# Head attention of a four-layer graph kernel: keys prepared before queries, and the head-stacking copies spread over three DMA queues

## What is computed

```
layer 0: three graph convolutions with layer norm       agg = adj^T (h W);  h = relu(LN(agg + b + h))
layer 1: additive attention (GAT)                        softmax(a . relu(q_i + k_j) + mask) @ h
layer 2: head attention, 4 heads of 32
         Q = h Wq + bq,  K = h Wk + bk,  V = h Wv + bv
         S = Q K^T / sqrt(32) + (1 - adj) * -1e9         per head, 2048 x 2048
         out = softmax(S) V  (heads side by side) @ Wo + bo
layer 3: normalised adjacency                            D^-1/2 (A + I) D^-1/2 h B
```

## Time and profile before

| | us |
|---|---|
| median of 3 runs | 13312.75 (13290.18 to 13324.34) |
| the profiled execution, its own time | 13312.38 |
| its span, first to last instruction | 13310.6 |
| PE busy in the span | 12569.7 (94%) |
| DVE busy | 10012.5 (75%) |
| ACT busy | 9177.3 (69%) |
| POOL busy | 372.5 (3%) |

### The profile page before, as it was taken

How to read it: one execution, slowest core, us unless ns; L and a number is a source line. 1 busy time by engine, 2 the same in 40 slices (tenths; PEclk the granted TensorE clock), 3 DMA queues, 4 the chain that set the end, 5 groups by cost and what they waited for, 6 DMA issues and landing times.

```text
span 13310.6 us, 251575 instructions
## 1 busy us (share of the span) xinstructions
PE 12569.7 (94%) x110721; PEld 6208.8 (47%) x110721; DVE 10012.5 (75%) x13975; ACT 9177.3 (69%) x8953; POOL 372.5 (3%) x500
## 2 busy tenths in 40 slices
PE   8998999989999899998999989999899998999989
PEld 3333843338433384333843338433384334843348
DVE  4887748877488775887758877598765887658876
ACT  3886738867388673886638866388663886638866
POOL 0000000000000000000000000000000000000000
PEclk9999999999999999999999999999999999999999
DMA  1001210012100131001310013100130001300012
GB/s 71 17 20 45 96 64 17 20 45 103 57 17 20 45 105 55 17 20 48 111 45 17 20 48 118 38 20 17 52 122 31 20 17 52 131 23 20 17 54 88
DMA packets 126942, 647.66 MB, mean 49 GB/s; under 512 B 15264, under 2 KB 49824, under 8 KB 52128
## 3 DMA queue, kind: packets, MB, share of 16 engines
q1 hardware_dynamic: 92688, 420.78, 9.3%
q0 software_dynamic: 20880, 143.66, 3.0%
q10 hardware_dynamic: 12288, 67.13, 2.2%
HBM read 556.01 MB, written 8.39 MB: 42 GB/s over the span
## 4 chain that ended last, share of the span: by engine, by line
PE 88%; DVE 6%; ACTq 2%; DMA 2%; ACT 1%; issue 1%; POOL 0%; SPq 0%; DVEq 0%
PE ps L1013 50%; PE ps L997 10%; PE ps L1055 8%; PE ps L1068 4%; PE ps L1026 4%; PE ps L1046 4%; PE ps L1185 3%; PE ps L949 2%; ACTq L535 2%; DMA adj_ring<-in_adj 1%; PE ps L1173 1%; DVE E L673 1%; DVE E L674 1%; DVE E L675 1%; DVE PT L701 1%
## 5 line engine op out<-in xcount | busy, mean ns | idle before, releaser
L1013 PE MATMUL ps<-E,a_win 128*32 128x512 f32 x65536 | 7113.6, 594 | 72.2 <-DVE E L675 72.2
L1013 PEld LDWEIGHTS ps<-E,a_win 128*32 128x32 f32 x65536 | 2102.5, 110 | 4904.7 <-issue 4745.5
L432 ACT ACTIVATE E<-Q,ka 128x2048 f32<-128x2048 f32 x2048 | 4073.5, 1989 | 0.0
L673 DVE TENSOR_SCALAR E<-Q,kd 128x2048 f32<-128x2048 f32 x2048 | 2628.8, 1284 | 794.3 <-PE ps L1013 757.8
L431 ACT ACTIVATE E<-Q,ka 128x1024 f32<-128x1024 f32 x2048 | 2347.9, 1146 | 964.9 <-PE ps L1013 964.3
L674 DVE TENSOR_SCALAR E<-Q,kd 128x2048 f32<-128x2048 f32 x2048 | 2623.2, 1281 | 0.0
L675 DVE TENSOR_SCALAR E<-Q,kd 128x1024 f32<-128x1024 f32 x2048 | 1531.0, 748 | 0.0
L742 DVE CUSTOM_DVE_ANT_0 T<-ps,adj_ring 128x2048 f32<-128x2048 f32 x512 | 1173.3, 2292 | 237.5 <-PE ps L1046 211.1
L459 ACT ACTIVATE T<-T,nmin 128x2048 f32<-128x2048 f32 x512 | 1022.1, 1996 | 316.1 <-issue 313.6
L371 ACT ACTIVATE PT<-ps 128x512 f32<-128x512 f32 x1792 | 1001.0, 595 | 341.6 <-PE ps L1055 276.9
L1055 PE MATMUL ps<-ident,T 128*128 128x128 f32 x8192 | 1128.5, 281 | 12.3 <-ACT PT L371 5.4
(11 more groups left out here) (119 smaller groups left out, 7590.5 us busy)
## 6 DMA issues: line engine op xcount, KB each, us to landing
adj_ring<-in_adj SPq DMA_DIRECT2D x384, 1024.0 KB, 4.9
adj_res<-in_adj POOLq DMA_DIRECT2D x128, 1024.0 KB, 7.4
qst<-qh ACTq DMA_DIRECT2D x64, 256.0 KB, 7.0
qst<-ql ACTq DMA_DIRECT2D x64, 256.0 KB, 8.7
kst<-kh ACTq DMA_DIRECT2D x64, 256.0 KB, 5.2
kst<-kl ACTq DMA_DIRECT2D x64, 256.0 KB, 5.2
HW<-in_x POOLq DMA_DIRECT2D x9, 1024.0 KB, 12.3
X<-in_x SPq DMA_DIRECT2D x128, 64.0 KB, 1.9
```

The source lines that it names most:

```text
L432: nc.scalar.activation(E[:, s + 3, :], Q2[:, :], ACT.Relu, bias=ka[:, u, 48 + m:49 + m]).then_inc(e_act, 1)
L673: nc.vector.tensor_scalar(E[:, s, :], Q2[:, :], kd[:, u, m:m + 1], 0.0, ALU.add, ALU.max)
L1013: last = mm(ps[QROWS * grp:QROWS * (grp + 1), 4 * u + c, :], win, E[:, s + grp, c * CH:(c + 1) * CH], start=(m == 0), stop=(m == QUADS - 1 ...
```

## The change

- The keys are projected, evacuated and split before the queries. DVE splits the keys in four chunks of 512 columns as ACT evacuates them, and the queries in two parts: `FIRST`, columns 0 to 511 (the first four tiles), and `REST`, the other 1536.
- The 16 key copies move to SP's queue, behind a wait for the fourth key chunk (`k2_dve`) and behind the first two ring loads of the head attention. ACT's queue copies only `FIRST` of the queries (16 DMAs of 64 KB). POOL's queue copies `REST` (16 DMAs of 192 KB), and only then issues `fetch`.
- The first score waits for `FIRST` of the queries (`stq_first`), not for all; `stq_rest` is waited for before tile 4's queries are taken. The wait for `V` moves from before the first score to before the third.
- `qh` and `ql` no longer lie under `T2`; `T2`'s heads 0 and 1 lie over an unused space.
- The `bo` addition moves from DVE to POOL, behind `fetch`; DVE waits for it (`bo_rdy`) where it adds the attention's output.
- The next graph's statistics move from before the first score into tiles 6 to 9, one `bn_stats` a step, and the aggregation into tile 10.

```diff
+        def stack(eng, dst, parts, h, cols, done):
+            for blk in range(4):
+                eng.dma_start(dst[HD * blk:HD * (blk + 1), h, cols].bitcast(F32),
+                              parts[blk][HD * h:HD * (h + 1), cols].bitcast(F32)).then_inc(done, 16)
+        FIRST, REST = slice(0, CH), slice(CH, N)
...
+                        if phase == 1 and tt == 0:
+                            sp.wait_ge(k2_dve, (b + 1) * NC)
+                            for h in range(HEADS):
+                                stack(sp, kst, (kh, kl, kh, kl), h, slice(0, N), stk_in[h])
...
-                pool.wait_ge(qk2_dve, b * 2 + 1)
+                pool.wait_ge(q2_dve, (b + 1) * 2)
+                for h in range(HEADS):
+                    stack(pool, qst, (qh, qh, ql, ql), h, REST, stq_rest)
                 fetch(b + 1 if more else b)
+                pool.wait_ge(zn_rdy, (b + 1) * (HEV * NC))
+                nc.gpsimd.tensor_tensor(X[:, :, :], X[:, :, :], over_tiles(bo_b[:, :]), ALU.add).then_inc(bo_rdy, 1)
...
-                for dst, parts, k in ((qst, (qh, qh, ql, ql), 1), (kst, (kh, kl, kh, kl), 2)):
-                    act.wait_ge(qk2_dve, b * 2 + k)
-                    for h in range(HEADS):
-                        for blk in range(4):
-                            act.dma_start(...)
+                act.wait_ge(q2_dve, b * 2 + 1)
+                for h in range(HEADS):
+                    stack(act, qst, (qh, qh, ql, ql), h, FIRST, stq_first)
...
                     if h == 1 and not last:
+                        if t == TPC - 1:
+                            dve.wait_ge(stq_rest, (b + 1) * (16 * 16))
                         queries2(b, t + 1, 1 - u)
...
-                nc.vector.tensor_tensor(X[:, :, :], X[:, :, :], over_tiles(bo_b[:, :]), ALU.add)
-                for src, hi, lo, k in ((HW, qh, ql, 0), (AGG, kh, kl, 1)):
...
+                for c in range(NC):
+                    cols = slice(c * CH, (c + 1) * CH)
+                    dve.wait_ge(k2_act, b * NC + c + 1)
+                    nc.vector.tensor_copy(kh[:, cols], AGG[:, cols]).then_inc(k2_hi, 1)
+                    dve.wait_ge(k2_hi, b * NC + c + 1)
+                    nc.vector.tensor_tensor(kl[:, cols], AGG[:, cols], kh[:, cols].bitcast(F32), ALU.subtract
+                                            ).then_inc(k2_dve, 1)
+                for k, cols in enumerate((FIRST, REST)):
+                    dve.wait_ge(q2_act, b * NC + (1, NC)[k])
+                    nc.vector.tensor_copy(qh[:, cols], HW[:, cols]).then_inc(q2_hi, 1)
+                    dve.wait_ge(q2_hi, b * 2 + k + 1)
+                    nc.vector.tensor_tensor(ql[:, cols], HW[:, cols], qh[:, cols].bitcast(F32), ALU.subtract
+                                            ).then_inc(q2_dve, 1)
...
-                stats_next(b + 1)
-                dve.wait_ge(stq_in, (b + 1) * (16 * 16))
+                dve.wait_ge(stq_first, (b + 1) * (16 * 16))
...
+                            k = ((tt - 3) * 2 + u) * HEADS + h
+                            if 0 <= k < NT:
+                                stats_of_next(b + 1, k)
+                            if k == NT:
+                                aggregate_next(b + 1)
...
-                pe.wait_ge(v_sb, (b + 1) * NC)
-                pe.wait_ge(qk2_act, (b + 1) * 8)
+                pe.wait_ge(q2_act, (b + 1) * NC)
...
+                        if t * HEADS + h == 2:
+                            pe.wait_ge(v_sb, (b + 1) * NC)
                         step2(b, S0 + t * HEADS + h, t, h, t, t * HEADS + h)
```

More of the change, by code:

```diff
@@ L46 @@
 LN_MID = LN_COUNT - 2
-DVE_STEPS = 66
+DVE_STEPS = 64
 STEPS = NT * HEADS
@@ L157, in build @@
             PT2 = sb("PT2", [P, NC, CH], where=ph)
+            qh = sb("qh", [P, N], F32R, where=ph)
+            ql = sb("ql", [P, N], F32R, where=ph)
             with ExitStack() as sub:
@@ L160, in build @@
             with ExitStack() as sub:
-                qh = sb("qh", [P, N], F32R, where=sub)
-                ql = sb("ql", [P, N], F32R, where=sub)
+                T2_front = sb("T2_front", [P, 2, N], where=sub)
                 kh = sb("kh", [P, N], F32R, where=sub)
@@ L215, in build @@
         x2_rdy = sem("x2_rdy")
-        qk2_ps = sem("qk2_ps")
-        qk2_act = sem("qk2_act")
-        qk2_dve = sem("qk2_dve")
+        k2_ps = sem("k2_ps")
+        k2_act = sem("k2_act")
+        k2_hi = sem("k2_hi")
+        k2_dve = sem("k2_dve")
+        q2_ps = sem("q2_ps")
+        q2_act = sem("q2_act")
+        q2_hi = sem("q2_hi")
+        q2_dve = sem("q2_dve")
+        bo_rdy = sem("bo_rdy")
         v_ps = sem("v_ps")
         v_sb = sem("v_sb")
-        stq_in = sem("stq_in")
+        stq_first = sem("stq_first")
+        stq_rest = sem("stq_rest")
         stk_in = [sem(f"stk_in{h}") for h in range(HEADS)]
@@ L252, in build, with over_tiles @@
         block = ctx.enter_context(nc.Block())
+        def stack(eng, dst, parts, h, cols, done):
[3 more added lines that the diff above has]
+        FIRST, REST = slice(0, CH), slice(CH, N)
         def alone(eng):
             eng.sem_inc(waited, 1)
+        def over_tiles(row):
+            return row.rearrange("p (o d) -> p o d", o=1).broadcast_to([P, NT, D])
         def tcols(t):
@@ L408, in evac_q2, with evac_k2 @@
             def evac_q2(b, c):
-                act.wait_ge(qk2_ps, b * 8 + c + 1)
-                nc.scalar.activation(HW[:, c * CH:(c + 1) * CH], ps[:, 4 + c, :], ACT.Identity,
-                                     bias=bqs_c[:, 0:1], scale=-SCALE).then_inc(qk2_act, 1)
+                act.wait_ge(q2_ps, b * NC + c + 1)
+                nc.scalar.activation(HW[:, c * CH:(c + 1) * CH], ps[:, c, :], ACT.Identity,
+                                     bias=bqs_c[:, 0:1], scale=-SCALE).then_inc(q2_act, 1)
+            def evac_k2(b, c):
+                act.wait_ge(k2_ps, b * NC + c + 1)
+                nc.scalar.activation(AGG[:, c * CH:(c + 1) * CH], ps[:, 4 + c, :], ACT.Identity,
+                                     bias=bk_c[:, 0:1]).then_inc(k2_act, 1)
             def degrees(b, t, T, half, u):
@@ L523, in _ @@
                 evac1(b * NT + NT - 1, 1)
-                h_section(b, 1, LAYERS, Hf, lambda c: evac_q2(b, c))
+                h_section(b, 1, LAYERS, Hf, lambda c: evac_k2(b, c))
                 for c in range(NC):
-                    act.wait_ge(qk2_ps, b * 8 + 4 + c + 1)
-                    nc.scalar.activation(AGG[:, c * CH:(c + 1) * CH], ps[:, c, :], ACT.Identity,
-                                         bias=bk_c[:, 0:1]).then_inc(qk2_act, 1)
-                for dst, parts, k in ((qst, (qh, qh, ql, ql), 1), (kst, (kh, kl, kh, kl), 2)):
-                    act.wait_ge(qk2_dve, b * 2 + k)
-                    for h in range(HEADS):
-                        for blk in range(4):
-                            act.dma_start(dst[HD * blk:HD * (blk + 1), h, :].bitcast(F32),
-                                          parts[blk][HD * h:HD * (h + 1), :].bitcast(F32)
-                                          ).then_inc(stq_in if k == 1 else stk_in[h], 16)
+                    evac_q2(b, c)
+                act.wait_ge(q2_dve, b * 2 + 1)
+                for h in range(HEADS):
+                    stack(act, qst, (qh, qh, ql, ql), h, FIRST, stq_first)
                 S0 = b * (NT * HEADS)
@@ L656, in tiles @@
                 return buf[:, :].rearrange("p (t d) -> p t d", t=NT)
-            def over_tiles(row):
-                return row.rearrange("p (o d) -> p o d", o=1).broadcast_to([P, NT, D])
             def keys(t, T, u, first):
@@ L808, in stats_next, with stats_of_next, aggregate_next @@
             def stats_next(n):
-                dve.wait_ge(xn_in, (n + 1) * 16)
-                XN = tiles(HW)
                 for t in range(NT):
-                    last = nc.vector.bn_stats(stats[:, t, :], XN[:, t, :])
-                last.then_inc(xn_bn, 1)
-                dve.wait_ge(xn_bn, n + 1)
+                    stats_of_next(n, t)
+                aggregate_next(n)
+            def stats_of_next(n, t):
+                if t == 0:
+                    dve.wait_ge(xn_in, (n + 1) * 16)
+                nc.vector.bn_stats(stats[:, t, :], tiles(HW)[:, t, :]).then_inc(xn_bn, 1)
+            def aggregate_next(n):
+                dve.wait_ge(xn_bn, (n + 1) * NT)
                 alone(dve)
@@ L915, in _ @@
                         xg = X[:, g * TPC:(g + 1) * TPC, :]
+                        dve.wait_ge(bo_rdy, b + 1)
                         last = nc.vector.tensor_tensor(xg, ps[:, 4 + g, :].rearrange("p (t d) -> p t d", d=D), xg,
@@ L1133, in _ @@
                 h_section(b, 1, LAYERS, lambda c: mm(
-                    ps[:, 4 + c, :], wq[:, :], HT[:, c * CH:(c + 1) * CH], start=True, stop=True).then_inc(qk2_ps, 1))
+                    ps[:, 4 + c, :], wk[:, :], HT[:, c * CH:(c + 1) * CH], start=True, stop=True).then_inc(k2_ps, 1))
                 for c in range(NC):
```

(5 more changed lines are left out.)

4 lines of the change are left out of this document (removed).

## The result

The changed kernel takes 13428.77 us (median of 4 runs, 13407.34 to 13444.71), the kernel before 13308.23 (4 runs on the same chip): ratio 1.0086, 95% interval 1.0074 to 1.0097. The medians are 120 us apart, 15 us a graph. The forecast was 13306, within 13225 to 13355: wrong, and outside its range. The profiled execution was the slowest of the four, with a span of 13442.9 us.

The account below looks back on a forecast made before the run. PE, busy 94% of the span, was taken as the bound, its waits for key copies as the place to save. First score +57 plus 18.3 us gave fifth score +75.3 against 76.0; times eight, -6 us: 13306, range 13225 to 13355.

Parts of the forecast that it names:

- The sharing: In the stacking, three queues take equal packet turns whatever the size; keys in at +54.5, first score at +58.2.
- rival 2: First score waits for nearly all stacking bytes, at +64.1; fifth at +82.4, +6.4 us a graph, 13363; chance 0.13.
- The rate: How fast engines carry the stacking: 212 GB/s within one half, 274 mixed; first score at +57 (55 to 59).
- mixed halves: Stacking copies reading both partition halves run at 274 GB/s, not 212, saving 2.3 us; half of that was taken.
- the loss side: Chance 0.15 of a result over 0.3% (40 us, 5 us a graph) slower than before.
- Rival 1: Queries get through the stacking early, first score about +41; keys then decide, -8 us a graph, 13249; chance 0.32.

Follow-up runs that it names:

- e1: The changed kernel, but POOL waits for all sixteen key copies to land before issuing REST and the fetch; 13273.34 us, ratio 0.9963 to the kernel before.
- e7: The changed kernel with ACT's and POOL's jobs swapped: POOL issues FIRST, then the fetch, and ACT issues REST; 13288.58 us, ratio 0.9976 to the kernel before.
- e5: As e3, but the key copies of heads 1 and 2 alternate in SP's queue; 13216.79 us, ratio 0.9921 to the kernel before.
- e4: The kernel before with only bo on POOL and the statistics in tiles 6 to 10, stacking untouched; 13324.94 us, ratio 1.0003.
- e3: The changed kernel, but SP alone issues head 0's keys, FIRST, other keys; POOL waits for the keys; 13220.16 us, ratio 0.9922 to the kernel before.
- e6: As e3, but ACT issues FIRST of heads 2 and 3 beside SP's of heads 0 and 1; 13173.66 us, ratio 0.9889 to the kernel before.

## Why the prediction was wrong

**The sharing: this step failed.** "That is one turn each, whatever the size" was read off one overlap and carried over to three queues. Between SP and ACT it is right: 386 to 342 packets in e1. POOL's queue is another matter: 325 packets to 143 and 128 in the changed kernel, 411 to 145 and 117 in e7.

The overlap that the forecast leaned on shows it, when its packets are counted in short stretches and not worked out from the whole. The queues of the kernel before, graph 2, from 4594 to 4604:

```profile
q10 hardware_dynamic: 232, 1.29, 60.0%
q0 software_dynamic: 271, 1.05, 39.8%
```

from 4596 to 4601:

```profile
q0 software_dynamic: 239, 0.96, 71.1%
q10 hardware_dynamic: 59, 0.30, 24.0%
```

and from 4597 to 4599:

```profile
q0 software_dynamic: 113, 0.46, 96.6%
q10 hardware_dynamic: 2, 0.01, 2.0%
```

The whole looks like near one for one, because ACT's queue has the engines to itself before the fetch flows and after most of it is through. In between the fetch took four packets for one. The forecast's working let the fetch flow 1.5 us after its issue and so gave it 11 us; its first packet came 3.5 us after the issue, at 4596.0, and 90% of its packets had started 5.2 us later. The stacking moved 1.29 MB in the ten microseconds, not 1.6. Graph 0 was read the wrong way round too: its fetch took longer, but drew 251 packets to the stacking's 186 from 1273 to 1283. In all eight graphs the first 244 packets of the fetch went beside only 41 to 161 of the stacking. So neither three queues nor a backlog of seventeen transfers is needed for the advantage; one transfer of POOL's beside one other queue has it.

The forecast quoted the Trainium skill for its rule ("DMA: Bandwidth & Descriptors", Queues, rings and completion order). But that section's packet is a bundle of some 9 to 17 descriptors, while the forecast took it for one packet of the profile; how the two relate, no run here shows. What the trace does show is that the fetch and the stacking did not change places packet by packet: 113 to 2 in 2 us are on average seven of the fetch's packets for each engine, with next to none of the other queue's between. A turn that carries more for POOL than for the others would fit all the counts; the size of a turn was not shown.

What it did to the order: the forecast had `FIRST` land "last but for `REST`", at +57.6. In fact it landed behind `REST` too, with the fetch. That is rival 2 ("If the turns favour POOL, `FIRST` lands with the end"), with its mechanism as written; it had been given 0.13, because SP would be "done by +55". By the forecast's own prices the order alone moves the first score from +57 to +64, seven of the twelve microseconds.

**The rate: a term mis-sized.** The other five are the rate. Rival 2's sum has 36.1 + 4.0 = 40.1 us for all 9.44 MB, which is 235 GB/s. From 1270 to 1314 the three queues moved 9.18 MB at 209 GB/s; at that rate 9.44 MB take 45.2 us. About 1.5 us of the difference stood in the rows before the change: there the bytes took 41.6 us (43.4 less 1.8), as the engines were not busy all the time. The rest is the price of a row. From 1276 to 1288 the 0.78 MB of SP are 95 rows of 8 KB and took 0.325 x 12 x 16 = 62.4 us of engine time, 0.66 each with the counting packets; POOL's 225 rows of 6 KB took 115.4, 0.51 each; ACT's 78 rows of 2 KB took 13.2, 0.17 each. The forecast had 0.56, 0.42 and 0.14. They are 18 to 22% dearer in this stretch, in which 2.32 MB took 12 us (193 GB/s). Why a row costs more was not shown.

The forecast had gone the other way, and taken 1.2 us off for mixed halves. Its reading of the earlier trace rows does not hold: in the stretch at 212 GB/s heads 1 and 2 met as well (ACT issued head 1's last key copy at 4620.54 and head 2's first at 4621.92, and such a copy is in flight for 6 us or more). e5 puts the gain at 4%, which is near the Trainium skill's 6% and far from the forecast's 274 to 212.

**The range.** The forecast gave the loss side 0.15 and ended the range at 13355, below its own rival 2 (13363). The fifth score's delay cost (87.7 - 76.0) x 8 = 94 us, where rival 2 had priced it at 51.

**What was right.** SP's first issue at +22.1; ACT at +24.5 (forecast 25.2), POOL at +28.3 (28.0). The fifth score 18.45 us after the first in graph 0 (18.9 in the mean), 18.3 forecast. No key wait of a minimum. SP's issues over at +51.9, before its ring load. ACT free for its first exp: it then waits 48.5 us for the minimum. `bo` takes 4.51 us on POOL, covered, and the statistics fit into tiles 6 to 10: e4 shows 1.0003 for both. "POOL's 16 issues delay only the fetch" was the sentence that hid the loss: they cost POOL 8 us, and took the engines from `FIRST`.

**Rival 1** (queries early, 13249) needs no luck with the sharing: e3 and e6 pass its time by keeping POOL's bytes back and ordering the rest by hand. The third minimum then waits for the keys, as it said: up to 6.1 us in e3, 5.2 in e6.

## What to carry to other kernels

Here, splitting a transfer over more queues added no bandwidth once the engines were full (209 GB/s with three queues, 203 to 219 with one or two); it only gave away the order. Between queues with equal turns the one with the smallest rows gets the fewest bytes, and POOL's queue, at its start, took more than its turns. Put what is needed first into one queue in the order of need, hold bulk that nobody waits for behind a semaphore until the urgent bytes are in, and let a second engine issue only where the issuing (0.6 us a copy) is the limit. Before trusting a rule of sharing, count the packets of each queue in short stretches of an overlap, in all graphs, and if there is one, in an overlap with as many queues as the change will have.

## What was not expected of the hardware

POOL's queue drew more packets than SP's or ACT's during its first 5 to 12 us: four for one beside ACT's in the kernel before (239 to 59), 2.3 and 2.5 in graph 0 of the changed kernel, 2.8 and 3.5 in that of e7. Later in the same overlap it was about one for one (254 to 248 and 255). What ends the advantage was not tried.

In e1 POOL's addition of `bo` ran while DVE had to copy `qcur`, and the copy took 4.34 us instead of 0.43:

```profile
1303.49 4.57 POOL L388 TENSOR_TENSOR X<-X,bo_b 128x2048 f32<-128x2048 f32 x1
...
1304.02 4.34 DVE L756 CAST qcur<-qst 128x512 fp32r<-128x512 f32 x1
```

It ends with the addition, within 0.3 us. This happens in all eight graphs of e1 (4.3 to 5.6 us), and the third minimum stands right behind the copy: it comes 13.6 us after the first score, against 11.7 in the changed kernel, which is some 15 us of e1's time. In e4 the addition fell on the cast of the keys, which took 6.06 us instead of the 1.23 of the queries' cast:

```profile
1273.30 6.06 DVE L891 CAST kh<-AGG 128x2048 fp32r<-128x2048 f32 x1 [1.09 <-ACT AGG L535]
```

There nothing was lost, as the sixteen query copies were still ahead of the keys in the queue. The Trainium skill states the rule behind this: VectorE and GpSimd share one pair of ports, held by one of them for a whole instruction ("SBUF — State Buffer", Who interferes with whom). In the changed kernel the addition fell into DVE's long wait, and in e6 beside minima, which it did not lengthen (2.29 us), so neither paid for it.
